# A new order of the pieces beside the scans: the table LINE of a Mamba, adapter and expert kernel

## The reference, cut to what matters

```python
xz = einsum('bld,ed->ble', hidden, in_proj_w); x, z = split(xz, 2)      # 1024 channels each
xc = silu(sum(conv1d_w[:, k] * xp[:, k:k + l, :] for k in range(4)))
x_dbl = einsum('bld,ed->ble', xc, x_proj_w)                            # 128 ranks, 16 of B, 16 of C
delta = softplus(einsum('blr,dr->bld', x_dbl[..., :R], dt_proj_w) + dt_proj_bias)
...
h = h * exp(delta_t * A) + (delta_t * x_t) * B_t;  y_t = sum_n h * C_t  # the scan over 64 tokens
y = (y + xc * D_param) * silu(z)
x = x + einsum('bld,ed->ble', y, out_proj_w)
```

## Time and profile before

| | us |
|---|---|
| median of 3 runs | 1850.55 |
| lowest and highest | 1850.34, 1851.46 |
| profiled execution, its own time | 1850.99 |
| its span | 1848.9 |
| DVE busy in the span | 1436.8 (78%) |
| PE | 1661.9 (90%) |
| POOL | 1056.0 (57%) |
| ACT | 828.9 (45%) |

### The profile page before, as it was taken

The page is one execution under the profiler, slowest core; times in us unless marked ns, Lnnn a source line. Parts: engine busy times, 40 slices in busy tenths (PEclk is TensorE's granted clock), DMA queues, the critical chain, the costliest instruction groups (busy, mean ns, idle before and its releaser), DMA issues. The chain is left out here.

```text
span 1848.9 us, 28706 instructions
## 1 busy us (share of the span) xinstructions
PE 1661.9 (90%) x8052; PEld 1212.6 (66%) x8052; DVE 1436.8 (78%) x1917; ACT 828.9 (45%) x1248; POOL 1056.0 (57%) x832
## 2 busy tenths in 40 slices
PE   8668877989998999988787998999999999999997
PEld 5255544665555655555454647778789999989997
DVE  3699999999999999999999924777365566565654
ACT  2656765657767567765664511000122323232321
POOL 0288679887699885898888570000044434344443
PEclk9878989999999999989999999999999999999999
DMA  5121212133332322322213433112156565656664
GB/s 130 35 62 58 71 52 71 53 92 80 85 103 76 91 80 70 112 88 63 75 52 109 140 121 114 69 68 84 43 132 174 134 176 137 161 130 159 148 168 70
DMA packets 130024, 181.95 MB, mean 98 GB/s; under 512 B 21443, under 2 KB 79555, under 8 KB 126788
## 3 DMA queue, kind: packets, MB, share of 16 engines
q1 hardware_dynamic: 109540, 131.85, 22.2%
q0 software_dynamic: 17888, 43.79, 12.2%
q10 hardware_dynamic: 2432, 4.33, 0.9%
HBM read 276.18 MB, written 37.36 MB: 170 GB/s over the span
## 5 line engine op out<-in xcount | busy, mean ns | idle before, releaser
L1198 POOL TENSOR_TENSOR arena_kept<-arena_kept,b_all 128x512 f32<-128x512 f32 x512 | 636.7, 1274 | 239.9 <-DMA b_all<-bt_scratch 124.2
L1094 DVE TENSOR_TENSOR_SCAN arena_kept<-da,arena_kept 128x512 f32<-128x512 f32 x512 | 596.8, 1204 | 16.9 <-issue 7.0
L934 ACT ACTIVATE da<-arena_kept,a_neg 128x504 f32<-128x504 f32 x512 | 345.4, 685 | 221.2 <-DVE arena_kept L1094 214.1
L723 PE MATMUL hT<-ident_kept,arena_kept 128*128 128x128 f32 x2048 | 312.9, 297 | 137.0 <-DVE yacc L1106 68.5
L723 PEld LDWEIGHTS hT<-ident_kept,arena_kept 128*128 128x128 f32 x2048 | 251.8, 152 | 243.9 <-DVE arena_kept L1094 151.6
L1106 DVE SCALAR_TENSOR_TENSOR yacc<-hT,c_now,yacc 128x512 f32<-128x512 f32 x480 | 332.1, 732 | 8.9 <-PE hT L723 8.0
L2111 POOL DMA_INDIRECT out<-y,slots_kept x76 | 134.4, 1768 | 228.0 <-issue 162.5
L516 PE MATMUL bank<-hid,wt 128*128 128x512 f32 x512 | 239.1, 613 | 0.7 <-ACT hid L759 0.7
L516 PEld LDWEIGHTS bank<-hid,wt 128*128 128x128 f32 x512 | 97.3, 200 | 102.2 <-issue 101.3
L1981 ACT ACTIVATE gs<-egp 128x352 f32<-128x352 f32 x73 | 33.8, 464 | 238.8 <-PE eup L1291 238.2
L1743 POOL DMA_DIRECT2D slots_kept<-lists_kept x1 | 0.6, 567 | 214.4 <-DVE lists_kept L1695 214.4
(11 more groups left out here) (239 smaller groups left out, 3210.5 us busy)
## 6 DMA issues: line engine op xcount, KB each, us to landing
w_up_kept<-in_up_T SPq DMA_DIRECT2D x76, 1408.0 KB, 6.4
w_dn_kept<-in_dn_T SPq DMA_DIRECT2D x76, 768.0 KB, 7.7
b_all<-bt_scratch SPq DMA_DIRECT2D x128, 256.0 KB, 3.6
wt<-in_in_T SPq DMA_DIRECT2D x64, 256.0 KB, 2.9
wt<-in_out_T SPq DMA_DIRECT2D x32, 256.0 KB, 3.0
res<-in_x_pad SPq DMA_DIRECT2D x16, 256.0 KB, 4.2
x_scratch<-res SPq DMA_DIRECT2D x16, 256.0 KB, 2.1
wt<-in_w_T SPq DMA_DIRECT2D x16, 256.0 KB, 3.0
```

The lines of the kernel that those rows point to most:

```text
L723: mm = nc.tensor.transpose(turned_in(j, m, t)[:, d * P:(d + 1) * P], h[:, m % RING, d, t * P:(t + 1) * P], ident[:])
L934: nc.scalar.activation(out[:, :, 1:], rows[:, :, 1:], ACT.Exp, scale=a_neg[:, d, n:n + 1]) \
L1094: nc.vector.tensor_tensor_scan(h[:, n % RING, i, :], da[i % RING][:], dbx[:, i, :], 0.0, ALU.mult, ALU.add).then_inc(scan_done, 1)
L1198: nc.gpsimd.tensor_tensor(dbx[:, i, :], u[:, d, :], b_all[:, m % RING, :], ALU.mult) \
```

## The change

The 32 entries of LINE are replaced by another 32. Every piece is there once in both, and no other line of the kernel changes. So every engine gets the same work (the skip term stays a product with the identity into PSUM), in another order, and with other neighbours in the banks and slots. Entries of steps 16 to 20 in the diff, with the rest cut:

```diff
 LINE = [
...
     (["turn0"], ["x4"]),
-    (["x5"], ["silu0", "w0"]),
-    (["x6"], ["z4"]),
-    ([], ["x7", "gate0", "xr1"]),
-    (["w1", "gate1"], ["silu1", "rank0", "gate2"]),
...
+    (["silu0"], ["x5", "z3"]),
+    (["x6"], ["zsilu0", "x7"]),
+    (["w0", "silu1", "rank0"], []),
+    (["rank1", "xr3"], ["dt0", "gate0"]),
...
```

More of the change, by code:

```diff
@@ L44 @@
 LINE = [
[L45 to L60, removed]
-    (["turn0"], ["x4"]),
-    (["x5"], ["silu0", "w0"]),
-    (["x6"], ["z4"]),
-    ([], ["x7", "gate0", "xr1"]),
-    (["w1", "gate1"], ["silu1", "rank0", "gate2"]),
[L66 to L75, removed]
+    (["turn1", "gate4", "gate5"], []),
+    (["gate6", "z0"], ["cond0", "gate7"]),
+    (["out0"], []),
+    (["out1"], ["dt4"]),
+    (["out2"], []),
+    (["out3"], ["ln4", "cond1"]),
+    (["out4"], []),
+    (["out5"], ["dt5"]),
+    (["cond2"], ["ln5", "z1"]),
+    (["dt6"], ["dt7", "cond3"]),
+    (["ln6", "out6"], []),
+    (["out7"], []),
+    (["xr0", "x0"], ["skip0", "ln7"]),
+    (["x1", "z2"], []),
+    (["skip1", "xa", "x2"], ["xr1", "xr2"]),
+    (["x3"], ["skip2", "skip3"]),
+    (["turn0"], ["x4"]),
+    (["silu0"], ["x5", "z3"]),
+    (["x6"], ["zsilu0", "x7"]),
+    (["w0", "silu1", "rank0"], []),
+    (["rank1", "xr3"], ["dt0", "gate0"]),
+    (["w1"], ["gate1"]),
+    (["gate2", "w2"], ["ln0"]),
+    (["w3", "gate3"], ["row0", "dt1"]),
+    (["pre0", "bc0"], ["ln1"]),
+    (["z4"], ["bc1", "pre1"]),
+    ([], ["lg"]),
+    (["dt2"], ["ln2", "pre2", "row1"]),
+    (["z5"], ["dt3"]),
+    (["z6", "row2"], ["row3"]),
+    (["ln3", "pre3", "ct"], ["z7", "zsilu1"]),
     ([], []),
```

## The result

The changed kernel takes 1863.76 us (median of 5 runs, 1859.63 to 1870.92) against 1850.55 of the kernel before on the same chip (5 runs, 1846.31 to 1854.75): 1.0068 times before, 95% interval 1.0047 to 1.0089. It is slower, by 13 us. The profiled execution took 1863.5 us with a span of 1861.5, 12.6 more than before's span. The forecast was 1854.0 with the range 1844 to 1864, and slower as the likeliest case. So the sign held and the value was ten too low. The time lies above the 1849 to 1859 that the forecast gave its sum, and only 0.2 us inside the whole range. The question is where the ten come from.

A forecast was written before the change was run, and what follows sets the result against it. DVE was taken to bound the state-space blocks, its 24.3 us of idle time the ceiling of any gain. Losses of 15.1 against gains of 12.0 gave +3.1 on 1850.99: 1854 us, range 1844 to 1864.

The forecast's parts named there:

- three stalls of steps 18 to 20, less 3 x 1.18: Blocks 0 to 2: DVE loses 2.1, 1.05 and 1.4 (0.8 in block 0); 3.5 of old waits go; +9.5 us.
- x5 and z3 on PE, step 18 of block 1: In a row on PE, about 1.4 too late for the fourth addition, but hidden under the 2.1 loss before it.
- block 3, steps 16 to 20 (skips, zsilu0): Skip products cost 2.5 and 0.5, the moved Silu shows 1.0; 4.1 against 2.2 before: +2 us.
- out0 ahead of the turning: Step 2: out0 moves ahead of the turning but waits for POOL's last gate, 0.3 x 3: +0.9 us.
- clock in light steps, step 28: Blocks 1 and 2, lighter PE steps: half a chance of 1.4 in each, plus 0.2 x 3 at step 28: +2 us.
- step 10, blocks 1 and 2: With cond2 and cond3 a step apart, waits of 2.45 in block 1 and 2.0 in block 2 go: -4.5 us.
- steps 5 to 9 and 13, blocks 1 and 2: Given for steps 5 to 8: out1 ends 0.7 earlier and ln4 comes two steps later: -1.9 us in two blocks.
- starts of blocks 1 to 3: z6 and z7 in steps 29 and 30 keep PE's clock up at the blocks' ends: 1.2, 0.9 and 0.8, -2.9 us.
- block 3, steps 5 to 12: Given for steps 5 to 11 of block 3: 1.2 of 3.4 us of waits gained.
- Stalls sharing one cover: Rival: after 2.1 at step 18 the 1.05 and 1.4 may vanish, and out0's 0.9 too: 1846 us; chance 0.18.
- PE as the bound of the dense steps, with 1862: Rival: steps 13, 14, 19, 28; low clock in two places per block costs DVE 8 us: 1862; chance 0.20.
- the 8 that the forecast named as a sign: The forecast is wrong if DVE's waits for PE in the dense steps sum to over 8.

The follow-up runs named there:

- a transplant: Kernel before, with silu0 moved to the first list of step 17 and x7 to the second list of step 18: 1.0123 times before.
- the spaced kernel: Changed kernel with the crowded steps 17 to 21 spread as in the kernel before, one convolution per step: 1.0018 times before.
- the last one: Kernel before with cond2 and cond3 a step apart (steps 8 and 9) and z7 in the second list of step 30: 0.9969, 1847.1 us.

## Why the prediction was right in sign and ten too low

By its own steps, in DVE's idle time (36.5 less 24.3 is 12.2, and the lines below sum to it):

| step of the forecast | forecast | measured |
|---|---|---|
| three stalls of steps 18 to 20, less 3 x 1.18 | +9.5 | 11.7 - 3.5 = +8.2 |
| x5 and z3 on PE, step 18 of block 1 | 0 | +0.9 |
| block 3, steps 16 to 20 (skips, zsilu0) | +2 | 6.8 - 2.2 = +4.6 |
| out0 ahead of the turning | +0.9 | 0.47 + 1.96 + 2.16 = +4.6 |
| clock in light steps, step 28 | +2 | in the line above |
| block 0: z0, steps 12 and 13, its end | +0.2 | -0.2 |
| step 10, blocks 1 and 2 | -4.5 | -4.4 |
| steps 5 to 9 and 13, blocks 1 and 2 | -1.9 | 2.1 - 1.6 = +0.5 |
| starts of blocks 1 to 3 | -2.9 | 5.2 - 4.8 = +0.4 |
| block 3, steps 5 to 12 | -1.2 | 1.2 - 3.4 = -2.2 |
| block 3, steps 29 and 30 | -1.0 | -0.1 |

**The three stalls were right** in place and nearly in size: 2.28 (forecast 2.1), 0.73 (1.05), 1.07 (1.4; 0.55 in block 0, 0.8). Each came from adding ACT's rows in the new order and comparing with the time at which a scan wants its decay. Spacing them out gave 9.3 us back, and putting two of them into the kernel before made it slower. The conv_sum term was a third too high: it was taken from the row of 1.02 ahead of the blocks, where the seven waits run 1.02, 1.10 four times, 1.93 and 0.73 in both kernels; the last, 0.73, is what stands in the steps. What the forecast let lie under the first stall, x5 and z3 on PE, did so in blocks 0 and 2; in block 1, at the lower clock, 0.93 showed.

**The gain at the block's end failed.** The forecast counted the products behind z7 that run at full clock and not z7 itself, nor what stands behind z7: zsilu1. The row of z7 says 5.08 where 3.60 is a tile at full clock, because the clock had fallen before it. With ACT's copy, two table loads and the Silu in a row behind it, the decays of block 1 come 3.6 later than in before, and the wait is 1.72 instead of 1.24. Then POOL, which waits for a scan before its gates, sets step 2: 1.14, 1.13 and 0.89, where 0.4 was. The forecast mentioned that second limit and gave no figure for it. z7 alone, in before's order ahead of the Silu but with before's neighbours, found the clock up (its tile took 3.60) and did take the 1.24 away.

**out0 was mis-sized**: 0.3 a block for waiting on POOL's last gate, where 0.47, 1.96 and 2.16 came. The 0.47 is the term as meant; the rest is the clock, since PE had just waited 1.56 to 2.27 for that gate, and the tile behind took 5.2 to 5.4. The forecast priced exactly this, 1.4 for a light step, but put it elsewhere and with half a chance.

**Steps 5 to 9 failed**: b_all came no earlier, since SP stood behind out1 even longer, as out1 is behind the late out0. The forecast had out1 end 0.7 earlier.

**Step 10 came out by luck in part.** The 4.4 us of two waits are gone as forecast, but two kernels with the old step 10 had none there either.

**Block 3 was too cheap.** 2.34 behind the skips (2.5 forecast) and 1.18 for zsilu0 (1.0) were right. Not in the sum were 1.94 before the third scan of step 16, where ACT's first copy of a turned sum waits for PE ahead of the decays, and 0.95 for PE in step 18. The clock has a part in both. With z3 moved from step 14 to 17, PE has less to do ahead of the turning, and its first identity products took 3.05 at a granted clock of 0.69, where before had 1.88 at 1.00. All seven kernels with z3 at step 17 have the first wait: 0.61 to 0.78 where these products took 1.88, 1.89 to 2.09 where the clock was low; the seven with z3 at step 14 have none. And z3 itself took 4.75 in step 18, at 0.50.

**The rivals.** Stalls sharing one cover: no, all three came in every block, the first two at full size, the third with 0.55 in block 0 and 1.07 in the others. PE as the bound of the dense steps, with 1862, came nearest in number and is not what happened: in the dense steps DVE waited for PE 0.93 and 0.95 in step 18 of blocks 1 and 3 and 1.03 and 0.73 in steps 28 and 29 of block 3, 3.6 together, well below the 8 that the forecast named as a sign. What lost time on PE is a long tile at the low clock that follows a wait, in the light steps above all. That the time landed near a rival's number would have hidden this without the single waits. (The forecast counted 31 waits in the earlier trace rows; the rows sum to 39.)

## What to carry to other kernels

When pieces are reordered beside a saturated engine, add the follower engine's rows between two things that engine needs, at each place: this found 8 of the 12 us here within a few tenths, a repair gave as much back, and a transplant showed two of the stalls again. Before counting a gain, follow it one step on to the next engine that becomes last (here POOL's gates, SP's wait and the Silu behind z7): of 12.0 us of forecast gains the 4.8 of the block starts and of steps 5 to 9 turned into a loss of 0.9. A wait seen in one execution is looked for in a second before its removal is counted: the two at step 10 were absent from two traces whose step 10 had not changed. A repair is tried with its neighbours in view, since silu0 behind the decays or x7 beside z4 only changed which engine was late.

## What the runs showed of the hardware that was not expected

- The same eight matmuls of 128x512 took 3.67, 5.16 and 5.37 us in three blocks of one execution, and 6.72 in another; and in the projection to ranks 3.70 after an idle time of 2.21 and 6.73 after one of 2.58. Windows of 5 us over the slow ones show a granted clock of 0.66 (345 to 350), 0.66 (850 to 855), 0.50 (345 to 350 of the spaced kernel) and 0.51 (250 to 255 of the last one), over the fast tile 1.00. The same idle time of PE, 1.56, stood ahead of 3.67 and of 5.16. Behind out0 DVE waited 0.47 to 3.52 us. That such places also move the medians is likely and wasn't shown.
- A Silu with its two table loads costs ACT 4.5 us at every place, and the next decay starts 1.29 us after the last load began: nothing else is lost to the load.
- DVE's copy of C, 128x64, took 0.69 and 0.71 us in the changed kernel's blocks 2 and 3, where it took 0.20 in before. POOL's rows tell when: the copy ends with the POOL product that is under way. Block 2:

```profile
580.76 3.74 POOL L1198 TENSOR_TENSOR arena_kept<-arena_kept,b_all 128x512 f32<-128x512 f32 x3
...
582.63 0.69 DVE L1124 COPY c_now<-c_next 128x64 f32<-128x64 f32 x1
```

The second of the three products ends at about 583.25, the copy at 583.32. In all fourteen traces every such copy of more than 0.20 us, up to 1.32, ends within 0.1 us of the end of a POOL product. No run tried this by itself.
